# Expert layers: all 32 row fetches issued first, blocks turned by groups, first products by pairs, results copied by fours

## The reference

```python
# first: probs = softmax(x @ Wr + br); each token takes its two best of 8 experts,
#        each expert keeps at most cap tokens, by gate
#        y = gate * (silu(x @ W1[e] + b1[e]) @ W2[e] + b2[e])
logits = jnp.einsum('nc,ec->ne', xf, router_w)          # second
probs = jax.nn.softmax(logits, axis=-1)
top_w, top_i = jax.lax.top_k(probs, TOP_K)
top_w = top_w / jnp.sum(top_w, axis=-1, keepdims=True)
h = jax.nn.gelu(jnp.einsum('nc,ech->enh', xf, w1), approximate=False)   # C=128 -> H=512
y = jnp.einsum('enh,ehc->enc', h, w2)
out = jnp.einsum('ne,enc->nc', comb, y)
```

## Time and profile before

| | |
|---|---|
| time, median of 3 runs | 1128.98 us |
| the profiled execution, from first to last instruction (its span; its own time is told by this alone) | 1166.7 us |
| first expert layer, first fetch to last send, in the trace | 202.1 to 332.3 us |
| second expert layer, the same | 1034.8 to 1149.3 us |
| PE busy, whole span | 1021.1 us (88%) |
| POOL busy, whole span | 291.8 us (25%) |

### The profile page before, as it was taken

The page is one execution under the profiler, slowest core; times in us unless marked ns, Lnnn a source line. Parts: engine busy times, 40 slices in busy tenths (PEclk is TensorE's granted clock), DMA queues, the critical chain, the costliest instruction groups (busy, mean ns, idle before and its releaser), DMA issues.

```text
span 1166.7 us, 22431 instructions
## 1 busy us (share of the span) xinstructions
PE 1021.1 (88%) x8264; PEld 490.1 (42%) x8268; DVE 846.9 (73%) x1585; ACT 796.1 (68%) x1174; POOL 291.8 (25%) x296
## 2 busy tenths in 40 slices
PE   9747667777888789999999999999999999977785
PEld 6412224777864322332223223232223332447785
DVE  3599997255334789999999999999999991361123
ACT  3653432445555569999999999999999999332122
POOL 0079871555325410000000000000000000036652
PEclk9969998898899889999999999999999999989898
DMA  3055533644123420011100111001111000066333
GB/s 106 1 188 185 194 108 110 199 123 121 55 89 117 143 72 19 17 35 34 35 22 15 35 35 35 19 18 35 35 34 20 17 4 5 3 193 204 116 94 124
DMA packets 57975, 87.94 MB, mean 75 GB/s; under 512 B 26240, under 2 KB 28664, under 8 KB 57484
## 3 DMA queue, kind: packets, MB, share of 16 engines
q1 hardware_dynamic: 51694, 75.52, 21.0%
q0 software_dynamic: 4544, 9.32, 2.6%
q10 hardware_dynamic: 1630, 1.67, 0.5%
HBM read 73.10 MB, written 12.94 MB: 74 GB/s over the span
## 4 chain that ended last, share of the span: by engine, by line
PE 68%; DVE 10%; issue 9%; DMA 4%; ACT 3%; another core or an unknown queue 2%; POOL 2%; SPq 1%; ACTq 0%; DVEq 0%; POOLq 0%
PE psum L959 24%; PE psum L945 22%; PE psum L1084 6%; PE psum L1070 6%; PE psum L949 2%; DVE ssm_h L1738 2%; PE psum L1053 1%; PE psum L789 1%; DVE tile_max L2018 1%; DMA w1r<-y_dram 1%; POOL h0T L1457 1%; DVE ssm_g L1747 1%; PE psum L769 1%; DVE proj_o L2014 1%
## 5 line engine op out<-in xcount | busy, mean ns | idle before, releaser
L1320 ACT ACTIVATE probs<-psum 128x1024 f32<-128x1024 f32 x512 | 505.5, 1041 | 15.1 <-PE psum L949 4.1
L2018 DVE TENSOR_REDUCE tile_max<-psum 128x1 f32<-128x512 f32 x720 | 456.3, 684 | 27.9 <-PE psum L945 26.4
L959 PE MATMUL psum<-probs,v_head 128*32 128x256 f32 (+1 forms) x3840 | 320.8, 406 | 0.7 <-ACT probs L1320 0.4
L945 PE MATMUL psum<-k_stack,q_stack 62*128 62x512 bf16 x994 | 311.2, 397 | 10.9 <-DMA q_stack<-q_dram 7.4
L949 PE MATMUL psum<-q_stack,k_stack 64*128 64x512 bf16 x1024 | 302.8, 384 | 4.1 <-DMA q_stack<-max_parts 3.7
L945 PEld LDWEIGHTS psum<-k_stack,q_stack 62*128 62x128 bf16 x994 | 92.1, 110 | 245.6 <-DVE tile_max L2018 116.5
L1509 POOL TENSOR_TENSOR max_parts<-row_max,no_shift 128x8 bf16<-128x8 f32 x32 | 6.4, 199 | 537.9 <-DVE row_max L1994 537.9
L959 PEld LDWEIGHTS psum<-probs,v_head 128*32 128x32 f32 x3840 | 75.7, 108 | 154.6 <-issue 102.9
L1084 PE MATMUL psum<-w_held,hid 128*128 (+1 forms) x624 | 92.6, 296 | 25.2 <-ACT hid L1379 11.2
L1070 PE MATMUL psum<-x_cols,w1r 128*128 128x128 f32 (+1 forms) x624 | 92.2, 296 | 10.3 <-issue 7.7
L1084 PEld LDWEIGHTS psum<-w_held,hid 128*128 128x128 f32 x624 | 83.7, 208 | 28.4 <-issue 27.2
(11 more groups left out here) (284 smaller groups left out, 1074.8 us busy)
## 6 DMA issues: line engine op xcount, KB each, us to landing
w1r<-w SPq DMA_DIRECT2D x78, 256.0 KB
ssm_b<-bc_dram SPq DMA_DIRECT2D x32, 512.0 KB, 4.1
k_stack<-k_dram SPq DMA_DIRECT2D x60, 120.0 KB
w_held<-w SPq DMA_DIRECT2D x16, 256.0 KB, 4.4
w1r<-y_dram SPq DMA_DIRECT2D x16, 256.0 KB, 5.2
q_stack<-q_dram SPq DMA_DIRECT2D x30, 96.0 KB
bc_p<-bc_dram SPq DMA_DIRECT2D x5, 512.0 KB, 5.7
xtok_dram<-x_tok SPq DMA_DIRECT2D x8, 256.0 KB, 2.4
```

The lines of the kernel that those rows point to most:

```text
L945: mm(bank, queries, k_stack[rows, u, keys:keys + C], start=True, stop=True).then_inc(s1_ps, 1)
L959: i = mm(psum[32 * j:32 * j + VM, 7, lo:hi], v_head[:, u, kt, :], probs[:, kt % 4, j * C + lo:j * C + hi], start=kt == 0, stop=kt == KT - ...
L1320: f(probs[:, kt % 4, hf * HALF:(hf + 1) * HALF], banks(2 * slot, 2), ACT.Exp, scale=SCALE).then_inc(p_ready, 1)
L2018: v.tensor_reduce(top, bank, AX.X, ALU.max).then_inc(s1_read, 1)
```

## The change

Items are taken in units of two (20 units, the last of one), blocks are turned in groups (2, 2, then seven of 4), results are copied in sets of four items (10 sets).

```diff
-XG_RING = 8
-OT_RING = 6
-GATES_TURNED = 30
-COUNT_LATER = 2
+UNITS = [(i, min(i + 2, ITEMS)) for i in range(0, ITEMS, 2)]
+NU = len(UNITS)
+TURNS = [(0, 2), (2, 4)] + [(i, i + 4) for i in range(4, BLOCKS, 4)]
+ROW_SETS = [(i, min(i + 4, ITEMS)) for i in range(0, ITEMS, 4)]
+HID_RING = 4
+TURN_BANK, GATE_BANK, ROW_BANK = 4, 5, 6
+SPREAD_UNITS = (1, 2)
+COUNT_LATER = 3
+def turned_in(u):
+    return [g for g, (first, _) in enumerate(TURNS) if first // 2 == u]
@@ buffers @@
-        x_got = sparse_sb("x_got", [128, XG_RING, 128])
-        o_rows = sparse_sb("o_rows", [128, OT_RING, 128])
+        last_rows = sparse_sb("last_rows", [128, ITEMS - 2 * TILES, 128])
+        first_rows = lane_hot[:].rearrange("p k l s -> p (k l s)").bitcast(F32).rearrange("p (i d) -> p i d", d=128)
+        def o_rows(first, end):
+            held, before = ((first_rows, 0), (y_sum, TILES), (last_rows, 2 * TILES))[first // TILES]
+            return held[:, first - before:end - before, :].rearrange("p i d -> p (i d)")
@@ PE @@
+                def turn(g):
+                    first, end = TURNS[g]
+                    pe.wait_ge(got[g], 16 * (end - first) * (layer + 1))
+                    if layer or g:
+                        pe.wait_ge(cols_ready, layer * NT + g)
+                    for i in range(first, end):
...
+                def up(u):
+                    unit = layer * NU + u
+                    if unit >= 2:
+                        pe.wait_ge(hidden_ready, unit - 1)
+                    for i in range(*UNITS[u]):
...
+                def down(u):
...
+                    pe.wait_ge(hidden_ready, unit + 1)
+                    if at == 0 and rows >= 2:
+                        pe.wait_ge(o_rows_ready, rows - 1)
...
                 turn(0)
                 up(0)
                 turn(1)
-                for i in range(ITEMS):
-                    if i + 2 < BLOCKS:
-                        turn(i + 2)
-                    if i + 1 < ITEMS:
-                        up(i + 1)
-                    down(i)
-                    if layer == 0 and 1 <= i <= NC:
-                        spread_gates(i - 1)
...
+                up(1)
+                turn(2)
+                for u in range(NU):
+                    for g in turned_in(u + 3):
+                        turn(g)
+                    if u + 2 < NU:
+                        up(u + 2)
+                    if layer == 0 and u in SPREAD_UNITS:
+                        spread_gates(2 * SPREAD_UNITS.index(u))
+                    down(u)
+                    if layer == 0 and u in SPREAD_UNITS:
+                        spread_gates(2 * SPREAD_UNITS.index(u) + 1)
+                    if layer == 0 and 0 <= u - COUNT_LATER < ROUNDS:
+                        count_round(u - COUNT_LATER)
+                if layer == 0:
+                    gates_turned()
@@ ACT, first layer @@
+                for u in range(NU):
+                    hidden(0, u)
...
+                    for g in turned_in(u + 3):
+                        columns(g)
+                    if u in SPREAD_UNITS:
+                        for c in range(2):
+                            spread(2 * SPREAD_UNITS.index(u) + c)
+                    if u and u % 2 == 0:
+                        rows(u // 2 - 1)
+                rows(NR - 1)
@@ POOL @@
                 def get(i):
-                    if n >= XG_RING:
-                        pool.wait_ge(turned_ps, n - XG_RING + 1 + (TILES if i >= XG_RING and layer else 0))
-                    g.indirect_dma_start(x_got[:, k, :], None, xtok_dram,
+                    g.indirect_dma_start(x_cols[:, i, :], None, xtok_dram,
...
                 def send(i):
-                    pool.wait_ge(o_rows_ready, n + 1)
+                    pool.wait_ge(o_rows_ready, layer * NR + i // 4 + 1)
...
-                for i in range(XG_RING):
+                for i in range(BLOCKS):
                     get(i)
                 for i in range(BLOCKS):
                     send(i)
-                    if i + XG_RING < BLOCKS:
-                        get(i + XG_RING)
                 pool.wait_ge(place_ready, placed(layer)["more"])
+                pool.wait_ge(put, 16 * (layer * ITEMS + BLOCKS))
                 for i in range(BLOCKS, ITEMS):
                     send(i)
```

More of the change, by code:

```diff
@@ L110, with turn_of @@
 FIRST_Q_LOADS = 6
+def turn_of(i):
+    return next(g for g, (first, end) in enumerate(TURNS) if first <= i < end)
+def turned_in(u):
+    return [g for g, (first, _) in enumerate(TURNS) if first // 2 == u]
 def placed(layer):
@@ L717, in sparse @@
                     if n >= W_RING:
-                        sp.wait_ge(hidden_ps, n - W_RING + 1)
+                        before, at = divmod(n - W_RING, ITEMS)
+                        sp.wait_ge(hidden_ps, before * NU + at // 2 + 1)
                     sp.dma_start(w1r[:, k, :], w1_all[bass.ds(e, 1)].rearrange("o p f -> (o p) f")).then_inc(w1_in[k], 16)
-                for k in range(OT_RING):
-                    sp.wait_ge(put[k], 16 * len(range(k, (layer + 1) * ITEMS, OT_RING)))
+                sp.wait_ge(put, 16 * (layer + 1) * ITEMS)
                 for c in range(NC):
@@ L1044, in sparse @@
             def sparse(layer):
[L1045 to L1070, removed]
-                    j.then_inc(hidden_ps, 1)
@@ new lines, in down @@
+                    for i in range(*UNITS[u]):
+                        e = pe.value_load(tile_expert_i[0:1, i:i + 1], min_val=0, max_val=NE - 1) if i < BLOCKS else i - BLOCKS + 1
+                        space = psum[:, ROW_BANK + rows % 2, i % 4 * 128:(i % 4 + 1) * 128]
+                        for hc in range(HC):
+                            weights = w2_held[:, bass.ds(e, 1), hc, :].rearrange("p o d -> p (o d)")
+                            j = mm(space, hid[:, unit % HID_RING, i % 2, hc, :], weights, start=hc == 0, stop=hc == HC - 1)
@@ L1344, in attention, with hidden @@
                 store_chunks(act, NH - 1, LAST_BY_ACT)
[L1346 to L1349, removed]
-            def silu_blocks():
[L1353 to L1362, removed]
+            def hidden(layer, u):
+                unit = layer * NU + u
+                act.wait_ge(hidden_ps, unit + 1)
+                if unit >= HID_RING:
+                    act.wait_ge(rows_ps, layer * NR + max((u - HID_RING) // 2 + 1, 0))
@@ L1364, in spread @@
                 def spread(c):
                     act.wait_ge(gates_ps, c + 1)
-                    f(chunk(gates_rep, c), psum[:, 3, :], ACT.Identity).then_inc(gates_step, 1)
-                columns(0)
-                columns(1)
+                    f(chunk(gates_rep, c), psum[:, GATE_BANK, :], ACT.Identity).then_inc(gates_step, 1)
+                for g in range(3):
+                    columns(g)
                 act.wait_ge(bias_ready, 1)
[L1371 to L1379, removed]
-                    j.then_inc(hidden_ready, 1)
-                    if i:
-                        rows(i - 1)
-                    if i + 2 < BLOCKS:
-                        columns(i + 2)
-                    if 2 <= i <= NC + 1:
-                        spread(i - 2)
@@ L1394, in weigh @@
+                rows(NR - 1)
+            def gelu_blocks():
+                for u in range(NU):
+                    unit = NU + u
+                    first, end = UNITS[u]
+                    hidden(1, u)
+                    f(hid[:, unit % HID_RING, 0:end - first].rearrange("p i h s -> p (i h s)"), banks(2 * (unit % 2), end - first),
+                      ACT.Gelu).then_inc(hidden_ready, 1)
             def weigh(layer):
```

122 lines of the change are left out of this document (75 added, 47 removed).

## The result

The changed kernel takes 1139.09 us (median of four runs, 1135.90 to 1145.93), the kernel before 1128.82 beside it: a ratio of 1.0101, 95% interval 1.0065 to 1.0136. Run again beside its mended versions it came to 1.0097 (1.0060 to 1.0133). It is slower by one per cent, 10 to 11 us; the forecast was 8.4 us slower, 1137.

What follows compares the result with a forecast made beforehand. It took the chain through PE's products as the bound in the expert layers, with POOL's issue pace slower for 24 items; second layer 0, first layer +5.0 and clock +3.4 gave +8.4 on 1129.0, 1137 us, range 1132 to 1143.

Steps and rivals of the forecast that it cites:

- Late marks: Both expert layers: ACT and DVE go on late after PE's products, 47 us in the trace, taken as absent from timed runs.
- the faster rival: Both expert layers: late marks are in timed runs too and three quarters of 47 us are saved, 1102 us; chance 0.23.
- 9.3 us around the span and in what the sum leaves out: Whole kernel: gap between the 1119.7 span without late marks and the 1129.0 timed median, taken as equal for both kernels.
- Second layer, 0: Second expert layer: last sends end at 1129.2 against 1130.5 before; taken as 0 us, ends -2 and +3.
- First layer, +5.0: First expert layer: PE's added waits on ACT move the end from 304.1 to 309.1, 5.0 us slower.
- the clock, +3.4: First layer: half clock for 3.4 us behind each of two PE waits loses 1.7 us each; ends 0 and +6.8.
- turn, ACT's 512-wide copy of 0.60 and marks, one unit: 220.9: Start of first layer: after fetch 7 lands at 215.6, turn, copy and PE's first unit are done by 220.9.
- The two waits forecast: First layer: PE idle 3.2 and 2.9 us behind the second and fourth spread, until ACT's Silu is done.
- The sum for the kernel before, 304.1: First layer before the change: end at 304.1 by its own paces without late marks, where the trace has 332.3.
- What costs nothing: Expert layers: ten wide copies for 39 narrow ones, hidden beside PE, and weights given back by two, add no time.
- The expert's number: Both expert layers: loading it between two downs of one unit, from -1 to +4 us a layer, taken as 0.
- The marks named in advance: Expert layers: signs of a right forecast, such as 32 unbroken fetches in 40 us, and of a wrong one.

Runs made afterwards that it cites:

- mended versions: Changed kernel with spreads one to a unit, ACT's first Silu ahead of the third copy, and rows by twos, singly 1.0061, 1.0075, 1.0081, together 1.0011.
- the version with spreads apart: Changed kernel with the four gate spreads one behind each down of units 1 to 4, counting products begun at unit 6: ratio 1.0061.
- the spare products: Changed kernel with 24 (first layer) and 20 (second) spare products ahead of PE's first turn instead of 10: ratio 1.0093.

## Why the prediction was right, and where its steps failed

*Late marks belong to the recorded execution.* Right: two more recordings have none, and the faster rival falls with them. But they do not come with every recording, so the rule that the prediction cited (the Trainium skill, NOTIFIC — the notification-queue block, section 7.1 on overflow: a full queue can hold back the engine) would have to say what filled it in one recording of three; no run here shows that.

*9.3 us around the span and in what the sum leaves out.* Wrong. Time and span differ by 1.8 us (1135.90 and 1134.1) and 1.9. The 1119.7 without late marks lies inside what the kernel before does: its further recordings have 1119.1 and 1129.0. What lies between that and the median is how executions differ, 6.3 of these 9.9 us in the first layer, by its clock; the timed runs went from 1117.9 to 1134.8.

*Second layer, 0.* The lengths forecast were 95.7 before (1034.8 to 1130.5) and 94.4 after; 94.4 and 95.5 came, each the mean of two recordings. One us more, inside the ends of -2 and +3. The landing wait was not the last thing there: DVE's rows were (1108.33).

*First layer, +5.0, and the clock, +3.4.* Before: 102.0 forecast from first fetch to last send, 100.0 and 106.3 measured. After: 107.0 and the clock, 110.4, against 113.1 and 112.3. The sum is near, partly by luck, since its terms were off both ways. The step that failed is "turn, ACT's 512-wide copy of 0.60 and marks, one unit: 220.9". It let PE go through up and down without ACT's order; the Silu of unit 0 stands behind the third turn's copy, PE waits 2.94 us and the clock falls behind that. With the layer's later start of 2.8 us (204.91 against 202.1) taken off, the first down ended at 225.8, 4.9 us late. Of that (rounded) 0.8 is the later start of the third turn (219.24, less 2.8, against 215.6), 2.3 lies between that turn and the up, and 1.7 is the clock behind it. The two waits forecast, 3.2 and 2.9, were 2.75 and 2.35. And of the two clock losses one came behind another wait than those named: at 237.60 the clock stayed, at 223.0 it fell. Two falls of 1.7 us were right in number; the version with spreads apart, which loses the waits of 5.1 us and one fall, gained 6.1 where 6.8 were due.

The clock's term has a flaw that its size hides. The sum for the kernel before, 304.1, has half clock in one place alone (5.0 us for three groups that take 2.7 at 0.89 each). But its further recordings have 4.0 and 17.5 us of it in that layer, and the changed kernel's has 13.7: two falls of 3.4, and 6.9 at the start, which no term had. With half of these times taken off, as an estimate, the layer is 98 us long in both recordings of the kernel before and 106 in the changed kernel's. So some 8 us are order and waits, where the forecast had 5.0 (PE's waits on `hid` alone are 8.0 against 0.9), and that the change costs clock as well is not shown.

*What costs nothing.* The weights given back by two showed no wait on PE, and the gates turned late were done before the last send (313.71 and 318.05). The wide copies did cost at the start: PE waits 0.75 us for each of the first two in the first layer (the row at 212.34 is one), and 2.5 us for three in the second. Behind the start it waits for none. The expert's number cost nothing: in steady state PE's up and down of a unit follow at 1.79 us each (285.71, 287.50, 289.29), twice the 0.89 of the earlier trace rows.

*The marks named in advance.* Fetches without a break until 246.2, 41 us: right. Waits of 3 us behind the second and fourth spread: right in place; half clock behind each: right for one. Last send 8 us behind PE's last down: 7.8 (310.23 to 318.05). A landing wait of 3 us: 3.00 in the first layer (309.42), but in the second, and in the first layer of the changed kernel's second recording, the rows came last. Second layer some 95 us: 95.9. One mark named for a wrong prediction came as well: in the first layer the sends find their rows late from the second set on, so there PE was behind, not POOL. The sum had let POOL wait there, at the end, so it went by PE's list already; its mark did not fit it.

## What to carry to other kernels

When products are grouped, read off for each engine what now stands ahead of the one instruction that the next group needs: here one copy ahead of the first Silu, and two copies of spread gates ahead of the Silu of each of two later units, made PE wait 8.0 us, and another order took nearly all of that away with products and turns still grouped. A set that is waited for at the end should be small: twos for fours took 2.4 us from the first layer in one recording. Do not count on grouping as such: mended, the kernel is level with the one before. Record the kernel before more than once: the first recording was nearly 40 us longer than the median of the timed runs, and two others were 9.9 us apart.

## What the runs showed of the hardware that was not expected

The clock's fall is not told by the length of a wait: it fell behind 2.94 and 2.35 us, not behind 2.75 between them, in both recordings of the changed kernel, and, with the spare products, behind 1.61 and 0.75. How much of a layer runs near half clock differs between executions of one program (4.0 and 17.5 us in the kernel before).

The fourth fetch of the first layer took 1.70 us in the changed kernel and 1.72 before, the others 0.94 to 1.26. DVE's copy beside it, in the changed kernel:

```profile
209.18 1.70 POOL L1573 DMA_INDIRECT x_cols<-xtok_dram,get_row  x1 [0.30 <-issue]
...
209.54 1.23 DVE L1888 COPY ln_xc<-rt_gate 128x2048 f32<-128x2048 f32 x1
```

The issue ended 0.11 us after the copy (210.88 and 210.77), and 0.12 in the second recording of the kernel before (208.55 and 208.43). The Trainium skill (SBUF — State Buffer, on two separate sides) says that such a copy locks POOL out of a port that it needs to write the transfer's descriptors, until the copy has ended; both kernels' traces agree in the times, and show no port.
